# Last feed-forward of a six-layer decoder: relu outputs of the first part kept in SBUF, every fourth group rounded on Pool, norms applied there

## The chip, the cores and the metric

One Trainium2 chip, one core. The metric is the device time of one launch in microseconds, the median of the runs. The core's engines are TensorE (PE; its weight loads stand as PEld in the profile), VectorE (DVE), ScalarE (ACT), GpSimd (Pool, POOL in the profile) and SyncE (SP), which issues the DMAs. They run side by side and wait for one another through semaphores.

## The reference

Six residual layers with a layer norm behind each, on x of 8 batches by 256 rows by 512. The change is in the last of them, a feed-forward with emulated fp8:

```python
def _fp8_matmul(x2d, w):
    scale_x = jnp.maximum(jnp.max(jnp.abs(x2d)) / FP8_MAX, 1e-06)
    scale_w = jnp.maximum(jnp.max(jnp.abs(w)) / FP8_MAX, 1e-06)
    x8 = (x2d / scale_x).astype(jnp.float8_e4m3fn)
    w8 = (w / scale_w).astype(jnp.float8_e4m3fn)
    out = jnp.matmul(x8.astype(x2d.dtype), w8.astype(x2d.dtype).T)
    return out * (scale_x * scale_w)
...
h = _fp8_matmul(x2d, w_fc)
h = jnp.square(jax.nn.relu(h))
out = _fp8_matmul(h, w_proj)
...
x = _layernorm(x + _L1_ffn_ref(x, L1_ffn_w_fc, L1_ffn_w_proj), axis=-1)
```

x2d has 2048 rows and 512 columns, w_fc gives 2048 hidden units, w_proj brings them back to 512 columns. Each product scales by one maximum over its whole input. So the maximum over all of h must be known before the first element of h can be rounded for the second product.

## The kernel before

The layers run one after another; `fp8_ffn_1` is the last. Its weights have been rounded and turned earlier and lie parked in DRAM. It has two parts, each a block of programs, one per engine.

The **first part** finds the maximum of h. The largest element of x comes from a reduction across the partitions on Pool (L2265). Then x is rounded to e4m3 in eight batches of 256 rows: ACT writes `f_x_value` and `f_x_raised` (L2205, L2206), DVE rounds with two instructions (`round_x`, L1122 and L1124), PE turns the result (L2172), ACT copies it to `f_xT` (L2210). Four blocks of 512 rows follow, each of eight groups of 256 hidden units. For a group PE does eight matmuls of 512 columns into two PSUM banks (L2182), and DVE takes the maximum of the 128x1024 result straight from PSUM (L2237); nothing else of it is kept. PE has three bank pairs and waits until DVE has read one. DVE rounds two batches of the next block after the maxima of groups 1 and 4, and PE turns them after its groups 3 and 6. Behind the last group come another reduction across partitions on Pool (L2267) and a chain of one-column instructions on DVE that ends in the scale (L2245 to L2259).

The **second part** goes over the eight batches of 256 rows, with an order made by `slot` and counted out by the class `Plan`. For each group of 256 hidden units it multiplies again on PE (L596, called by `sum_products`), ACT takes the relu and two squares (`f_relu`, `f_value`, `f_raised`: L2316, L2321, L2322), DVE rounds with two instructions (`round_e4m3_above_zero`, L2089 and L2091) into `f_hidden`, and PE multiplies by w_proj (L2304) three groups later. At the end of a batch, for two tiles of 128 rows: DVE adds the product to x (L2345, called fin in the code), takes statistics (L163, L165), Pool makes the root of the variance (`norm_root`, L173 and L175), and DVE applies the norm (`norm_apply`, L180). A finished batch goes out by DMA (L2362).

The two rounding instructions are the same form in every place; the second waits for the first:

```python
    eng.scalar_tensor_tensor(tmp, raised, LEAST, value, ALU.max, ALU.subtract).then_inc(linked, 1)
    eng.wait_ge(linked, n + 1)
    return eng.scalar_tensor_tensor(out, raised, LEAST, tmp, ALU.max, ALU.subtract)
```

Both of its tensors, the bf16 `raised` and the fp32 `value` or `tmp`, lie in SBUF.

## Time and profile before

| | |
|---|---|
| median of 3 runs | 2402.31 us (2401.89 to 2404.9) |
| span of the profiled execution, first to last instruction | 2393.3 us |
| what lies around the span, by the median | 9.0 us |
| last feed-forward in the profiled execution | 2168.3 to 2393.3 us |
| its first part | 2168.3 to 2257.2 us |
| its second part, to the last instruction of DVE | 2257.2 to 2390.1 us |

One execution is profiled; it has no time of its own beside the span. All times of rows are microseconds from the start of that span. A row of a timeline has its start, its duration, the engine, the line of the kernel, the operation, what it writes and reads with the shapes, a count, and in brackets how long the engine had idled and who ended that. A name's buffer number is left out.

### The profile page before, as it was taken

To read this page: it belongs to the slowest core of one execution; us is meant where nothing else is said; L and a number is where in the kernel's file an instruction comes from. 1 tells how busy PE (TensorE), PEld (TensorE's weight loads), DVE (VectorE), ACT (ScalarE), POOL (GpSimd) and SP (SyncE) were. 2 spreads that over 40 slices of the span, in tenths; PEclk is the share of its full clock that TensorE was granted. 3 is DMA by queue.
4 is the path that set the end of the run, shared out by engine and by line. 5 is a ranking of instruction groups with operands and counts; after the bars stand their busy time and mean duration, and the time that the engine had idled before them with its cause. 6 is when DMAs were issued, how large, how long until landed. Compare 5 with 4: busy or idle time off the path is not lost. (4 is left out here: it accounts for less than half of the span.)

```text
span 2393.3 us, 40933 instructions
## 1 busy us (share of the span) xinstructions
PE 2087.9 (87%) x15408; PEld 1781.9 (74%) x15408; DVE 1641.9 (69%) x3731; ACT 1221.2 (51%) x3223; POOL 751.6 (31%) x810
## 2 busy tenths in 40 slices
PE   6999999379899888799978789999999999975897
PEld 5899988267777777577767688889988888962454
DVE  3677777547777776688856655566777676765798
ACT  3656655256766664333433244445555554432397
POOL 1222222376666763344430111111111112220012
PEclk8999999689999998899989899999999999997999
DMA  4111121200000000611110032223324221201001
GB/s 163 54 54 47 48 71 63 77 8 6 5 5 6 6 1 1 229 63 36 36 49 1 2 140 93 85 100 127 118 89 154 89 102 57 77 1 71 1 27 45
DMA packets 50875, 143.95 MB, mean 60 GB/s; under 512 B 4588, under 2 KB 15853, under 8 KB 45688
## 3 DMA queue, kind: packets, MB, share of 16 engines
q1 hardware_dynamic: 50680, 141.34, 16.7%
q8 instruction: 124, 2.03, 0.4%
q14 instruction: 71, 0.58, 0.1%
HBM read 111.95 MB, written 29.36 MB: 59 GB/s over the span
## 5 line engine op out<-in xcount | busy, mean ns | idle before, releaser
L2030 POOL TENSOR_TENSOR x_probs<-x_probs,x_total 128x512 f32<-128x512 f32 x128 | 133.2, 1041 | 588.4 <-DVE x_total L2000 588.2
L1951 ACT ACTIVATE x_probs<-x_probs,x_nmax 128x256 f32<-128x256 f32 x256 | 128.3, 502 | 259.3 <-DVE x_nmax L1990 259.3
L139 DVE TENSOR_TENSOR x_probsT_lo<-banks,x_probsT_hi 128x512 fp32r<-128x512 f32 x256 | 168.0, 682 | 51.8 <-ACT x_probsT_hi L133 51.3
L133 ACT ACTIVATE x_probsT_hi<-banks 128x512 fp32r<-128x512 f32 x256 | 144.9, 603 | 107.8 <-PE banks L1885 83.6
L596 PE MATMUL banks<-x_turned,x_wq_hi 128*128 128x256 f32 x1024 | 185.4, 282 | 9.8 <-DVE x_turned L139 9.8
L596 PE MATMUL banks<-x_probsT_hi,x_V_hi 128*128 128x256 f32 x512 | 151.5, 296 | 33.7 <-DVE x_probsT_lo L139 33.7
L596 PEld LDWEIGHTS banks<-x_turned,x_wq_hi 128*128 128x128 f32 x1024 | 157.0, 189 | 11.0 <-DVE x_turned L139 11.0
L901 POOL TENSOR_TENSOR x_probs<-x_probs,x_total 128x960 f32<-128x960 f32 (+1 forms) x128 | 131.7, 1049 | 92.9 <-DVE x_total L1053 92.9
L588 POOL TENSOR_TENSOR a_probs<-a_probs,a_total 128x512 f32<-128x512 f32 (+1 forms) x64 | 94.9, 1493 | 179.7 <-DVE a_total L558 179.7
L1010 ACT ACTIVATE x_probs<-banks,x_nmax 128x240 f32<-128x240 f32 x256 | 114.8, 467 | 68.6 <-DVE x_nmax L1041 68.6
L596 PE MATMUL banks<-x_probsT_hi,x_V_lo 128*128 128x256 f32 x512 | 147.3, 288 | 0.0
L596 PE MATMUL banks<-x_probsT_lo,x_V_hi 128*128 128x256 f32 x512 | 147.3, 288 | 0.0
L596 PE MATMUL banks<-x_turned,x_wq_lo 128*128 128x256 f32 x512 | 143.5, 280 | 0.0
L1308 POOL TENSOR_TENSOR f_hid_lo<-f_hid,f_hid_hi 128x256 fp32r<-128x256 f32 x128 | 93.9, 734 | 142.0 <-ACT f_hid_hi L133 141.8
L596 PEld LDWEIGHTS banks<-x_probsT_hi,x_V_hi 128*128 128x128 f32 x512 | 100.0, 195 | 43.2 <-DVE x_probsT_lo L139 41.2
L1289 ACT ACTIVATE f_act<-f_z 128x256 f32<-128x256 f32 x128 | 53.4, 417 | 151.1 <-DVE f_z L1360 151.0
L522 ACT ACTIVATE a_probs<-banks,a_nmax 128x128 f32<-128x128 f32 (+1 forms) x256 | 104.3, 425 | 39.9 <-DVE a_nmax L548 39.5
L1271 PE MATMUL banks<-f_downT,f_hid_hi 128*128 128x512 f32 x256 | 111.1, 434 | 1.6 <-POOL f_hid_lo L1308 1.6
L596 PE MATMUL banks<-x_wo_hi,x_oT_hi 128*128 128x512 f32 x256 | 105.0, 410 | 2.6 <-DVE x_oT_lo L139 2.6
L596 PE MATMUL banks<-x_wo_hi,x_oT_lo 128*128 128x512 f32 x256 | 101.0, 395 | 0.0
L596 PE MATMUL banks<-x_wo_lo,x_oT_hi 128*128 128x512 f32 x256 | 101.0, 395 | 0.0
L596 PEld LDWEIGHTS banks<-x_probsT_lo,x_V_hi 128*128 128x128 f32 x512 | 100.3, 196 | 0.9
(450 smaller groups left out, 7146.2 us busy)
## 6 DMA issues: line engine op xcount, KB each, us to landing
x_turned<-x_parked SPq DMA_DIRECT2D x24, 1536.0 KB, 6.6
x_parked<-x_turned SPq DMA_DIRECT2D x8, 1536.0 KB, 5.8
x_raw_q<-in_L_xattn_Wq_dram SPq DMA_DIRECT2D x5, 1024.0 KB, 5.2
x_raw_o<-in_L_xattn_Wo_dram SPq DMA_DIRECT2D x5, 1024.0 KB, 8.4
x_all<-in_x_dram SPq DMA_DIRECT2D x2, 2048.0 KB, 18.0
a_sign_raw<-in_L_ffn_W_g_dram SPq DMA_DIRECT2D x8, 512.0 KB, 3.7
f_parked<-a_sign_turned SPq DMA_DIRECT2D x16, 256.0 KB, 2.4
a_sign_raw<-in_L_ffn_W_u_dram SPq DMA_DIRECT2D x8, 512.0 KB, 3.7
```

The source lines that it names most:

```text
L133: return eng.activation(out, in_, ACT.Copy, scale=scale)
L139: return eng.tensor_tensor(out, in_, high.bitcast(F32), ALU.subtract)
L522: ins = eng.activation(probs[u % NP][:, r, 0:keys], banks[:, r, :], ACT.Exp, bias=nmax[:, u, r:r + 1], accum_out=total[:, u, r:r + 1])
L588: eng.tensor_tensor(probs[u % NP][:, :, 0:keys], probs[u % NP][:, :, 0:keys], total[:, u, :].unsqueeze(2).to_broadcast([P, G4, keys]), ALU ...
L596: ins = eng.matmul(out, lhs, rhs, start=start and n == 0, stop=stop and n == len(steps) - 1)
L901: ins = eng.tensor_tensor(tile, tile, total[:, u, n, :].unsqueeze(2).to_broadcast([P, G4, c1 - c0]), ALU.mult)
L1010: eng.activation(probs[u % NP][:, r, 0:MAIN], g.S[:, r, 0:MAIN], ACT.Exp, bias=nmax[:, u, r:r + 1], accum_out=total[:, u, 0, r:r + 1])
L1271: ins = eng.matmul(g.S[:, 2 * b.parity + t, :], h[:, t * P:(t + 1) * P], downT[:, m, :], start=m == 0 and n == 0, stop=m == HT - 1 and n == 1)
L1289: eng.activation(act[zb][:, :], z[zb][:, :], ACT.Silu).then_inc(silued, 1)
L1308: eng.tensor_tensor(hid_lo[buf][:, :], hid[buf][:, :], hid_hi[buf][:, :].bitcast(F32), ALU.subtract).then_inc(low, 1)
L1951: ins = eng.activation(probs[t][r][:, j, :], probs[t][r][:, j, :], ACT.Exp, bias=nmax[:, t, r, j:j + 1], accum_out=total[:, t, r, j:j + 1])
L2030: eng.tensor_tensor(probs[t][r][:, :, :], probs[t][r][:, :, :], total[:, t, r, :].unsqueeze(2).to_broadcast([P, 2, S]), ALU.mult).then_inc ...
```

## The change

`fp8_ffn_1` is written anew. In the first part ACT takes the relu of every group from PSUM into an SBUF tensor `kept` (128 KB of each partition), PE's banks are freed by that, and DVE takes its maximum from `kept`. The value of x is made by Pool instead of ACT. Both reductions across partitions are done with a diagonal, a matmul with ones and a maximum (`everywhere`) in place of Pool's. w_fc and w_proj share one tensor `weights`; w_proj is loaded at the end of the first part.

The second part has no up-projection. It goes over four blocks of 512 rows by eight groups of 128x1024. ACT squares twice from `kept`. DVE rounds six groups of eight with the same two instructions. Of groups 3 and 7 DVE only does the `max` with `LEAST` (in place, on bf16), and Pool does the two subtractions. Statistics of the block before are taken behind groups 1, 2, 4 and 5 (`FINS`), and Pool makes the root and also applies the norm; for the last block DVE applies it. The semaphores of the norms are shared by all layers, with counts that run on (`so_far`), which changes no order in the other layers.

```diff
-    def __init__(self, prologue, slots, epilogue, events, rings):
+    def __init__(self, prologue, slots, epilogue, events, rings, so_far):
-        total = {e: 0 for e in events}
+        total = {e: so_far.get(e, 0) for e in events}
...
-        gathered, rooting, rooted = g.sem("a1_variance_ready"), g.sem("a1_root_steps"), g.sem("a1_root_ready")
+        gathered, rooting, rooted = g.gathered, g.rooting, g.rooted
...
+    NG = HT // 2
+    NB = B * S // BANK
+    WIDE = 2 * BANK
+    TILES = BANK // P
+    RING = 4
+    FINS = {1: 0, 2: 1, 4: 2, 5: 3}
+    BY_POOL = (3, 7)
+    def pooled(k):
+        return k in BY_POOL
+    def by_pool(u):
+        return sum(pooled(v % NG) for v in range(u))
...
+        kept = sb("kept", [P, NB, NG, WIDE])
+        xT = sb("xT", [P, KD, B * S], BF16)
+        weights = sb("weights", [P, 2, NG * KD * P], BF16)
+        fc = [weights[:, h, :].rearrange("p (m k n) -> p m k n", k=KD, n=P) for h in range(2)]
+        proj = [weights[:, h, :].rearrange("p (c m n) -> p c m n", c=D // P, n=P) for h in range(2)]
         pairs = [g.S[:, 0:2, :], g.S[:, 2:4, :], g.R[:, 0:2, :]]
+        last = kept[:, NB - 1, :, :]
+        value = [last[:, i, :] for i in range(2)]
+        raised, rounded = ([last[:, at, :].bitcast(BF16)[:, i * WIDE:(i + 1) * WIDE] for i in range(2)] for at in (2, 3))
...
+                half = KD * P * NG
+                for h in range(2):
+                    eng.dma_start(weights[:, h, :], parked[:, h * half:(h + 1) * half]).then_inc(w_loaded[h], 16)
+                rows = parked[:, 2 * half:4 * half].rearrange("p (c m n) -> p c (m n)", c=D // P, m=HT)
+                for h in range(2):
+                    eng.wait_ge(up_full, (NB - 1) * NG + (h + 1) * NG // 2)
+                    eng.dma_start(weights[:, h, :].rearrange("p (c n) -> p c n", c=D // P),
+                                  rows[:, :, h * NG * P:(h + 1) * NG * P]).then_inc(w_loaded[h], 16)
...
                 def group(n, k):
                     use = n * NG + k
                     if use >= 3:
-                        eng.wait_ge(up_free, use - 2)
+                        eng.wait_ge(up_kept, use - 2)
+                    h, m = divmod(2 * k, NG)
                     for j in range(2):
-                        m = 2 * k + j
                         for kt in range(KD):
-                            ins = eng.matmul(pairs[use % 3][:, j, :], fcT[:, m, kt, :], xT[:, kt, n * BANK:(n + 1) * BANK],
+                            ins = eng.matmul(pairs[use % 3][:, j, :], fc[h][:, m + j, kt, :], xT[:, kt, n * BANK:(n + 1) * BANK],
                                              start=kt == 0, stop=kt == KD - 1)
                     ins.then_inc(up_full, 1)
+                def spread_top(n, bank):
+                    eng.wait_ge(topped, 3 * n - 1)
+                    eng.matmul(bank, ones[:, :], diag[:, :], start=True, stop=True).then_inc(spread, 1)
+                eng.wait_ge(filled, 1)
+                spread_top(1, g.S[:, 0, 0:P])
                 turn(0)
...
-                def scale_x(c):
+                def raise_x(c):
                     if c == 0:
                     if c >= 2:
                         eng.wait_ge(xrounded, c - 1)
-                    src = g.x[:, c * QT * D:(c + 1) * QT * D]
-                    eng.activation(value[c % 2][:, :], src, ACT.Copy, scale=w8.inverse[:, 0:1])
-                    eng.activation(raised[c % 2][:, :], src, ACT.Abs, scale=w8.raise_by[:, 0:1]).then_inc(valued, 1)
+                    eng.activation(raised[c % 2], x_of(c), ACT.Abs, scale=w8.raise_by[:, 0:1]).then_inc(raised_s, 1)
...
-                for c in range(B):
-                    scale_x(c)
-                    if c >= 1:
-                        copy_x(c - 1)
-                copy_x(B - 1)
+                raise_x(0)
+                raise_x(1)
+                copy_x(0)
+                copy_x(1)
+                raise_x(2)
+                raise_x(3)
+                for n in range(NB):
+                    for k in range(NG):
+                        use = n * NG + k
+                        eng.wait_ge(up_full, use + 1)
+                        eng.activation(kept[:, n, k, :], pairs[use % 3].rearrange("p j n -> p (j n)"), ACT.Relu).then_inc(up_kept, 1)
+                        if n < NB - 1 and k in (4, 6):
+                            copy_x(2 * n + 2 + (k == 6))
+                        if n < NB - 2 and k in (5, 7):
+                            raise_x(2 * n + 4 + (k == 7))
...
+                def everywhere(n, bank, top, source):
+                    eng.tensor_reduce(amax[:, top:top + 1], source, AX.X, ALU.max).then_inc(topped, 1)
+                    eng.wait_ge(topped, 3 * n - 2)
+                    eng.tensor_scalar(diag[:, :], g.ident[:, :], amax[:, top:top + 1], None, ALU.mult).then_inc(topped, 1)
+                    eng.wait_ge(spread, n)
+                    eng.tensor_reduce(scaled[:, top:top + 1], bank, AX.X, ALU.max).then_inc(topped, 1)
+                    eng.wait_ge(topped, 3 * n)
                 eng.wait_ge(w8.x_topped, B)
-                eng.tensor_reduce(amax[:, 0:1], w8.x_tops[:, :], AX.X, ALU.max).then_inc(topped, 1)
-                eng.wait_ge(reduced, 1)
+                everywhere(1, g.S[:, 0, 0:P], 0, w8.x_tops[:, :])
...
                 for use in range(total):
                     n, k = divmod(use, NG)
-                    eng.wait_ge(up_full, use + 1)
-                    eng.tensor_reduce(hmax[:, use:use + 1], pairs[use % 3].rearrange("p j n -> p (j n)"), AX.X,
-                                      ALU.max).then_inc(up_free, 1)
+                    eng.wait_ge(up_kept, use + 1)
+                    eng.tensor_reduce(hmax[:, use:use + 1], kept[:, n, k, :], AX.X, ALU.max).then_inc(up_max, 1)
                     if n < NB - 1 and k in (1, 4):
                         round_x(2 * n + 2 + (k == 4))
...
             def _(eng):
-                eng.wait_ge(topped, 1)
-                eng.partition_all_reduce(scaled[:, 0:1], amax[:, 0:1], P, RED.max).then_inc(reduced, 1)
-                eng.wait_ge(topped, 2)
-                eng.partition_all_reduce(scaled[:, 3:4], amax[:, 3:4], P, RED.max).then_inc(reduced, 1)
-        relu = [sb(f"relu{i}", [P, BANK]) for i in range(NZ)]
-        value = [sb(f"value{i}", [P, BANK]) for i in range(NZ)]
-        raised = [sb(f"raised{i}", [P, BANK], BF16) for i in range(NZ)]
-        tmp = [sb(f"tmp{i}", [P, BANK]) for i in range(NZ)]
+                eng.memset(ones[:, :], 1.0).then_inc(filled, 1)
+                for c in range(B):
+                    if c == 0:
+                        eng.wait_ge(w8.linked, 6)
+                    if c >= 2:
+                        eng.wait_ge(xrounded, c - 1)
+                    eng.tensor_scalar(value[c % 2], x_of(c), w8.inverse[:, 0:1], None, ALU.mult).then_inc(valued, 1)
+        turning = xT[:, :, :].rearrange("p k n -> p (k n)")
+        raised, hidden = ([turning[:, (first + i) * WIDE:(first + i + 1) * WIDE] for i in range(RING)] for first in (0, RING))
...
+        def accumulator(n, t):
+            return (g.S if n % 2 else g.R)[:, t, :]
+                for u in range(NB * NG):
+                    n, k = divmod(u, NG)
+                    if k == 0 and n >= 2:
+                    wait_rounded(eng, u)
+                    h, m = divmod(2 * k, NG)
+                    for t in range(TILES):
                         for j in range(2):
-                            ins = eng.matmul(g.S[:, 2 * b.parity + t, :], h[:, j, t * P:(t + 1) * P], projT[:, :, 2 * m + j, :],
-                                             start=m == 0 and j == 0, stop=m == HT // 2 - 1 and j == 1)
+                            at = j * BANK + t * P
+                            ins = eng.matmul(accumulator(n, t), hidden[u % RING][:, at:at + P], proj[h][:, :, m + j, :],
+                                             start=k == 0 and j == 0, stop=k == NG - 1 and j == 1)
                     ins.then_inc(downed, 1)
...
+                for u in range(NB * NG):
+                    group = kept[:, u // NG, u % NG, :]
+                    if u >= RING:
+                        wait_rounded(eng, u - RING)
+                    eng.activation(raised[u % RING], group, ACT.Square, scale=raise_root)
+                    eng.activation(group, group, ACT.Square, scale=root).then_inc(squared, 1)
...
+                links = 0
+                for u in range(NB * NG):
+                    n, k = divmod(u, NG)
+                    group, raise_to = kept[:, n, k, :], raised[u % RING]
+                    eng.wait_ge(squared, u + 1)
+                    if pooled(k):
+                        eng.tensor_scalar(raise_to, raise_to, LEAST, None, ALU.max).then_inc(capped, 1)
+                    else:
+                        eng.scalar_tensor_tensor(group, raise_to, LEAST, group, ALU.max, ALU.subtract).then_inc(linked, 1)
+                        links += 1
+                        if u >= RING:
+                            eng.wait_ge(downed, u - RING + 1)
+                        eng.wait_ge(linked, links)
+                        eng.scalar_tensor_tensor(hidden[u % RING], raise_to, LEAST, group, ALU.max, ALU.subtract).then_inc(rounded_v, 1)
+                    if n and k in FINS:
+                        fin(n - 1, FINS[k])
...
+            @block.gpsimd
+            def _(eng):
+                def root_of(n, t):
+                    done = TILES * n + t
+                    eng.wait_ge(gathered, before["stats"] + done + 1)
+                    norm_root(eng, rooting, before["rooting"] + POOL_ROOT_STEPS * done, st[t], 1e-5, g.minus_half[:, :]).then_inc(rooted, 1)
+                    eng.wait_ge(rooted, before["root"] + done + 1)
+                for u in range(NB * NG):
+                    n, k = divmod(u, NG)
+                    if pooled(k):
+                        group, raise_to, n_before = kept[:, n, k, :], raised[u % RING], by_pool(u)
+                        eng.wait_ge(capped, n_before + 1)
+                        eng.tensor_tensor(group, raise_to, group, ALU.subtract).then_inc(pool_linked, 1)
+                        if u >= RING:
+                            eng.wait_ge(downed, u - RING + 1)
+                        eng.wait_ge(pool_linked, n_before + 1)
+                        eng.tensor_tensor(hidden[u % RING], raise_to, group, ALU.subtract).then_inc(rounded_p, 1)
+                    if n and k in FINS:
+                        t = FINS[k]
+                        root_of(n - 1, t)
+                        norm_apply(eng, x_tile(n - 1, t), x_tile(n - 1, t), st[t]).then_inc(applied_p, 1)
+                for t in range(TILES):
+                    root_of(NB - 1, t)
...
+                for b in range(B):
+                    n, half = divmod(b, 2)
+                    if n < NB - 1:
+                        eng.wait_ge(applied_p, QT * (b + 1))
+                    else:
+                        eng.wait_ge(applied_v, QT * (half + 1))
```

POOL, second part, from its start to the second group 7. `f_xT` holds the buffers `raised` and `hidden`, `f_kept` the relu outputs, `f_st` the statistics. Before:

```order
L173 TENSOR_SCALAR f_st<-f_st 128x1
L175 TENSOR_TENSOR f_st<-f_st,minus_half 128x1
L173 TENSOR_SCALAR f_st<-f_st 128x1
L175 TENSOR_TENSOR f_st<-f_st,minus_half 128x1
```

Of the change:

```order
L2387 TENSOR_TENSOR f_kept<-f_xT,f_kept 128x1024
L2391 TENSOR_TENSOR f_xT<-f_xT,f_kept 128x1024
L174 TENSOR_SCALAR f_st<-f_st 128x1
L176 TENSOR_TENSOR f_st<-f_st,minus_half 128x1
L181 TENSOR_SCALAR x_all<-x_all,f_st 128x512
L174 TENSOR_SCALAR f_st<-f_st 128x1
L176 TENSOR_TENSOR f_st<-f_st,minus_half 128x1
L181 TENSOR_SCALAR x_all<-x_all,f_st 128x512
L2387 TENSOR_TENSOR f_kept<-f_xT,f_kept 128x1024
L2391 TENSOR_TENSOR f_xT<-f_xT,f_kept 128x1024
```

Pool had 32 small instructions in this part; it has 16 of 128x1024 and 12 of 128x512 besides.

DVE, second part, a stretch around the end of a group 7 and the first statistics of the block before. Before, at the end of a batch:

```order
L2089 SCALAR_TENSOR_TENSOR f_tmp<-f_raised,f_value 128x512
L2091 SCALAR_TENSOR_TENSOR f_hidden<-f_raised,f_tmp 128x512
L2345 SCALAR_TENSOR_TENSOR x_all<-banks,f_scaled,x_all 128x512
L163 BN_STATS f_st<-x_all 128x6
L165 BN_AGGR f_st<-f_st 128x2
```

Of the change, from the first `max` alone of a group 7 on:

```order
L2356 TENSOR_SCALAR f_xT<-f_xT 128x1024
L2358 SCALAR_TENSOR_TENSOR f_kept<-f_xT,f_kept 128x1024
L2363 SCALAR_TENSOR_TENSOR f_xT<-f_xT,f_kept 128x1024
L2358 SCALAR_TENSOR_TENSOR f_kept<-f_xT,f_kept 128x1024
L2363 SCALAR_TENSOR_TENSOR f_xT<-f_xT,f_kept 128x1024
L2343 SCALAR_TENSOR_TENSOR x_all<-banks,f_scaled,x_all 128x512
L164 BN_STATS f_st<-x_all 128x6
L166 BN_AGGR f_st<-f_st 128x2
```

Between the `max` of group 7 and the statistics that need that group's product now stand the two groups 0 and 1 of the next block.

ACT, first part, from the sixth relu of a block on (`f_kept<-x_all` is the raised x, in the last block's place). Before:

```order
L2205 ACTIVATE f_x_value<-x_all,f_inverse 128x1024
L2206 ACTIVATE f_x_raised<-x_all,f_raise_by 128x1024
L2210 ACTIVATE f_xT<-banks 128x4x256
```

Of the change:

```order
L2222 ACTIVATE f_kept<-banks 128x1024 x5
L2209 ACTIVATE f_xT<-banks 128x4x256
L2222 ACTIVATE f_kept<-banks 128x1024
L2205 ACTIVATE f_kept<-x_all,f_raise_by 128x1024
L2222 ACTIVATE f_kept<-banks 128x1024
L2209 ACTIVATE f_xT<-banks 128x4x256
```

The relus of the groups stand between PE and DVE, and between the copies that PE waits for.

## Rows read from the trace of the kernel before

**Rows 1.** Busy time by stretch: us, each engine's busy time (instructions), granted clock, DMA.

```profile
2189.30:2253.50 64.20, 60.77 (x304) 27.65 (x304) 52.27 (x45) 16.46 (x16) 0.00 (x0) 0.97 0.00 1
...
2261.50:2385.00 123.50, 113.77 (x750) 70.86 (x748) 113.84 (x184) 108.59 (x189) 22.40 (x28) 0.99 0.07 26
```

**Rows 2.** Timeline of all engines, start of the first part.

```profile
2168.33 0.16 DVE L2228 TENSOR_REDUCE f_amax<-f_x_tops 128x1 f32<-128x8 f32 x1 [0.33 <-PEq L1779]
...
2178.44 0.38 POOL L2265 PARTITION_ALL_REDUCE f_scaled<-f_amax  x1 [13.27 <-issue]
...
2179.42 1.15 ACT L2205 ACTIVATE f_x_value<-x_all,f_inverse 128x1024 f32<-128x1024 f32 x1 [23.79 <-DVE f_raise_by L1117]
```

**Rows 3.** Timeline of all engines, blocks of the first part.

```profile
2197.08 1.22 DVE L1124 SCALAR_TENSOR_TENSOR f_x_rounded<-f_x_raised,f_x_value 128x1024 bf16<-128x1024 bf16 x1
...
2198.45 0.61 PE L2172 MATMUL banks<-ident,f_x_rounded 128*128 128x128 bf16 x8 [0.34 <-DVE f_x_rounded L1124]
...
2236.47 15.70 PE L2182 MATMUL banks<-f_xT,f_fcT 128*128 128x512 bf16 x72
```

**Rows 4.** Instructions that write or read f_diag: duration ns min/median/max.

```profile
L1251 PE MATMUL banks<-f_diag,f_ones x32: 275/328/528, 968.7 to 1194.4; 128*128 128x128 f32 x32
L1345 DVE TENSOR_SCALAR f_diag<-ident,f_inv x16: 285/286/288, 967.5 to 1190.8; 128x128 f32<-128x128 f32 x16
```

**Rows 5.** Timeline of DVE, end of the first part and second part.

```profile
2254.14 0.16 DVE L2245 TENSOR_TENSOR f_scaled<-f_scale 128x1 f32<-128x1 f32 x1 [0.49 <-POOL f_scaled L2267]
...
2261.50 0.69 DVE L2089 SCALAR_TENSOR_TENSOR f_tmp<-f_raised,f_value 128x512 f32<-128x512 bf16 x1 [4.35 <-ACT f_raised L2322]
...
2282.15 0.74 DVE L2345 SCALAR_TENSOR_TENSOR x_all<-banks,f_scaled,x_all 128x512 f32<-128x512 f32 x1
...
2283.77 0.69 DVE L2089 SCALAR_TENSOR_TENSOR f_tmp<-f_raised,f_value 128x512 f32<-128x512 bf16 x1
```

**Rows 6.** Timeline of all engines, the last statistics and the last norm.

```profile
2385.08 0.75 DVE L2345 SCALAR_TENSOR_TENSOR x_all<-banks,f_scaled,x_all 128x512 f32<-128x512 f32 x1 [0.72 <-PE banks L2304]
...
2389.55 0.55 DVE L180 TENSOR_SCALAR x_all<-x_all,f_st 128x512 f32<-128x512 f32 x1 [0.77 <-POOL f_st L175]
```

**Rows 7.** Groups of Pool's instructions by form, whole span: busy us, mean ns.

```profile
L139 POOL TENSOR_TENSOR x_wdv_lo<-x_raw_d,x_wdv_hi 128x1024 fp32r<-128x1024 f32 x1 | 2.4, 2354 | 0.0
...
L779 POOL MEMSET x_bias<- 128x512 f32 x1 | 0.5, 524 | 0.9 <-POOLq L324 0.9
```

**Rows 8.** Timelines of Pool and of DVE at 60 us, first layer.

```profile
60.17 1.42 POOL L588 TENSOR_TENSOR a_probs<-a_probs,a_total 128x512 f32<-128x512 f32 x1 [7.32 <-DVE a_total L558]
...
60.01 0.68 DVE L541 TENSOR_SCALAR a_sign_of<-a_sign_raw 128x1024 bf16<-128x1024 f32 x1
60.73 1.94 DVE L543 SCALAR_TENSOR_TENSOR a_sign_of<-a_sign_raw,a_sign_of 128x1024 bf16<-128x1024 f32 x1
```

**Rows 9.** Timelines of Pool and of DVE at 466 us, second layer.

```profile
466.53 6.30 POOL L139 TENSOR_TENSOR x_wo_lo<-x_raw_o,x_wo_hi 128x2048 fp32r<-128x2048 f32 x1 [8.18 <-ACT x_wo_hi L133]
...
466.12 1.21 DVE L139 TENSOR_TENSOR x_wk_lo<-x_raw_kv,x_wk_hi 128x1024 fp32r<-128x1024 f32 x1
467.25 1.21 DVE L139 TENSOR_TENSOR x_wdk_lo<-x_raw_d,x_wdk_hi 128x1024 fp32r<-128x1024 f32 x1
```

**Rows 10.** Timelines of Pool and of DVE in the second part.

```profile
2287.57 0.99 POOL L175 TENSOR_TENSOR f_st<-f_st,minus_half 128x1 f32<-128x1 f32 x1
...
2287.45 0.69 DVE L2091 SCALAR_TENSOR_TENSOR f_hidden<-f_raised,f_tmp 128x512 bf16<-128x512 bf16 x1
2288.05 0.68 DVE L2089 SCALAR_TENSOR_TENSOR f_tmp<-f_raised,f_value 128x512 f32<-128x512 bf16 x1
```

**Rows 11.** Line 139 on DVE, one input in PSUM: duration ns min/median/max.

```profile
L139 DVE TENSOR_TENSOR x_probsT_lo<-banks,x_probsT_hi x256: 637/683/693, 513.8 to 2151.3; 128x512 fp32r<-128x512 f32 x128
```

**Rows 12.** Busy time by stretch, columns as in the first group.

```profile
2380.50:2383.90 3.40, 3.24 (x8) 0.99 (x8) 3.24 (x7) 0.00 (x0) 0.53 (x1) 0.51 0.00 0
```

**Rows 13.** Timeline of PE in that stretch.

```profile
2380.66 4.38 PE L2304 MATMUL banks<-f_projT,f_hidden 128*128 128x512 bf16 x12 [1.91 <-DVE f_hidden L2091]
```

More of the change, by code:

```diff
@@ L321, in self_attention_0 @@
                 "root": {"out": 1}, "link": {"rec": 1, "out": STATISTICS_STEPS, "fin": 1}},
-        rings={"R": (4, {kind: lambda *a, kind=kind: turn[(kind, *a)] for kind in ring}), "S": (1, {"score": lambda m, qt: 0})})
+        rings={"R": (4, {kind: lambda *a, kind=kind: turn[(kind, *a)] for kind in ring}), "S": (1, {"score": lambda m, qt: 0})}, so_far=g.norms_so_far)
     with ExitStack() as mem:
@@ L2141, in fp8_ffn_1 @@
         hlinked = g.sem("f1_hmax_link")
-        fc_loaded, proj_loaded = [g.sem(f"f1_parked_fc_loaded{m}") for m in range(2)], g.sem("f1_parked_proj_loaded")
-        topped, reduced, valued = g.sem("f1_top_ready"), g.sem("f1_top_reduced"), g.sem("f1_x_scaled")
+        w_loaded = [g.sem(f"f1_parked_loaded{h}") for h in range(2)]
+        topped, spread = g.sem("f1_top_ready"), g.sem("f1_top_spread")
+        valued, raised_s = g.sem("f1_x_scaled"), g.sem("f1_x_raised")
         xlinked, xrounded, turned, copied = (g.sem("f1_x_" + n) for n in ("link", "rounded", "turned", "copied"))
-        with ExitStack() as raws:
-            def ring(name, dt):
-                return [raws.enter_context(nc.sbuf_tensor(f"f1_x_{name}{i}", [P, QT * D], dt)) for i in range(2)]
-            value, raised, rounded = ring("value", F32), ring("raised", BF16), ring("rounded", BF16)
-            block = raws.enter_context(nc.Block())
+        last = kept[:, NB - 1, :, :]
@@ L2152, in _, with x_of @@
+        value = [last[:, i, :] for i in range(2)]
+        raised, rounded = ([last[:, at, :].bitcast(BF16)[:, i * WIDE:(i + 1) * WIDE] for i in range(2)] for at in (2, 3))
+        def x_of(c):
+            return g.x[:, c * QT * D:(c + 1) * QT * D]
+        with nc.Block() as block:
             @block.sync
@@ L2279, in fp8_ffn_1 @@
-        block = mem.enter_context(nc.Block())
-        @block.tensor
-        def _(eng):
-            def do(job, b):
-                kind, a = job[0], job[2:]
-                if kind == "up":
-                    m, = a
-                    if (count := plan.freed("R", "relu", b, "up", m)) is not None:
-                        eng.wait_ge(relued, count)
-                    bank = g.R[:, plan.buf("R", b, "up", m), :]
-                    for j in range(2):
-                        ins = sum_products(eng, bank[:, j * S:(j + 1) * S],
-                                           [(fcT[:, 2 * m + j, kt, :], xT[:, kt, b.columns(1, 0, S)])
-                                            for kt in range(KD)])
-                    ins.then_inc(full, 1)
-                if kind == "down":
-                    m, = a
-                    if (b.c, m) == (0, 0):
-                        eng.wait_ge(proj_loaded, 16)
-                    eng.wait_ge(rounded, plan.done("round", b, "up", m))
-                    h = hidden[plan.buf("H", b, "up", m)]
-                    for t in range(QT):
+                eng.memset(ones[:, :], 1.0).then_inc(filled, 1)
@@ new lines, in fp8_ffn_1 @@
+        st = [sb(f"st{t}", [P, 12]) for t in range(TILES)]
+        gathered, rooting, rooted = g.gathered, g.rooting, g.rooted
+        before = dict(g.norms_so_far)
+        squared, capped = g.sem("f1_square_ready"), g.sem("f1_raised_capped")
+        linked, pool_linked = g.sem("f1_link"), g.sem("f1_pool_link")
+        rounded_v, rounded_p = g.sem("f1_rounded_by_vector"), g.sem("f1_rounded_by_pool")
+        downed, summed, stats = g.sem("f1_down_added"), g.sem("f1_sum_ready"), g.sem("f1_stats_link")
@@ new lines, in fp8_ffn_1 @@
+        with nc.Block() as block:
+            @block.tensor
+            def _(eng):
+                for u in range(NB * NG):
+                    n, k = divmod(u, NG)
+                    if k == 0 and n >= 2:
+                        eng.wait_ge(summed, TILES * (n - 1))
+                    if u in (0, NG // 2):
+                        eng.wait_ge(w_loaded[u // (NG // 2)], 32)
+                    wait_rounded(eng, u)
+                    h, m = divmod(2 * k, NG)
+                    for t in range(TILES):
@@ new lines, in _ @@
+            @block.gpsimd
+            def _(eng):
+                def root_of(n, t):
[17 more added lines that the diff above has]
+                        norm_apply(eng, x_tile(n - 1, t), x_tile(n - 1, t), st[t]).then_inc(applied_p, 1)
+                for t in range(TILES):
+                    root_of(NB - 1, t)
```

174 lines of the change are left out of this document (55 added, 119 removed).

## Prediction

> **What bounds it now.** I read the busy time by stretch first, then the timelines at the two parts' starts and ends, then every place where Pool and DVE work side by side. In the first part PE bounds: 60.77 of 64.20 us [rows 1]. A block of 512 rows takes 15.70 us for its 72 matmuls [rows 3], 1.74 for a group's eight; DVE is busy for 52.27 and ACT for 16.46, so ACT has room. Ahead of it stands a dead stretch: DVE has the maximum per partition at 2168.49, Pool's reduction only starts at 2178.44 although nothing in the trace holds it but "issue", and ACT's first instruction comes at 2179.42 [rows 2]. In the second part no engine bounds alone: DVE 113.84, PE 113.77, ACT 108.59 of 123.50 us [rows 1]. The change takes half of PE's work away there and nothing of DVE's, so what counts is DVE, and what Pool's new work does to it.
>
> **First part.** *Start.* Before, 2168.33 to 2179.42 is 11.1 us [rows 2]. Now: maximum 0.16, diagonal 0.29, matmul 0.53 (slowest of its kind), the maximum of its 128 columns about as the diagonal, 0.29 [rows 4], handovers between engines estimated at 0.45 together, and from there to ACT's first instruction 0.6, as now from 2178.82 to 2179.42: 2.3 us. Minus 8.8. Nothing hides that stretch, so all of it comes off.
>
> *Relu in the way.* DVE's rounding of x stands behind the maxima of groups 1 and 4, and the maximum now waits for a relu instead of PE's end. The nearest row for a relu of 128x1024 is ACT's 1.15 [rows 2]; with a handover of 0.1 the rounding comes 1.25 later. PE already waits 0.34 for the rounding at a turn [rows 3], so there is no slack to absorb it: six turns, plus 7.5. The last maximum is as much later: plus 1.25. Together +8.75. Bounds: the third bank pair lets PE swallow half of it (+4.4), or an x copy on ACT ahead of the relu adds about 1.0 a turn (+14.8).
>
> *Value on Pool, 128x1024.* The trace has no such instruction. The nearest are 0.52 for a 128x512 memset, twice that 1.04, and 2.35 for a two-input 128x1024 [rows 7]. I take 1.04: the rounding is then late only by its relu; at 2.35 the first batch costs about 2.5 once more.
>
> *Second reduction.* DVE's own maximum takes 0.16 as at the start, it waits 0.49 for Pool's and goes on at 2254.14 [rows 5], about 0.7 with the start; the new way takes 1.55 by the terms of the first, and one more column instruction 0.2: +1.05. First part: −8.8 + 8.75 + 1.05 = **+1.0**.
>
> **Second part.** It takes 132.95 us now, from 2257.15, 4.35 ahead of DVE's first rounding [rows 5], to the end of the last norm at 2390.10 [rows 6].
>
> *A pair of roundings* of 128x1024: one takes 1.22 [rows 3], the second waits for the first (1.25 to its start), and an independent follower starts 0.09 before the end (0.69 long, next one 0.60 later [rows 10]): 1.25 + 1.14 = 2.39 a group. The `max` alone is nearest to the 0.68 of a 128x1024 conversion [rows 8], 0.6 net; 1.22 is its upper bound, four microseconds over the part.
>
> *Pool against DVE.* This is the term that decides. At 60 us a two-input DVE instruction took 1.94, not 1.22, and ended 1.08 after Pool's end, while Pool's 128x512 took 1.42 and ended 0.90 after DVE's previous end [rows 8]: one waited whole for the other, both ways. At 466 us Pool's 128x2048 stood through two DVE instructions, to 468.46, then took 4.37, so 2.19 for 128x1024 [rows 9]. A DVE instruction with one input in PSUM never shows it (637 to 693 over 256 of them [rows 11]). The rounding pair has two inputs in SBUF, and it stands right beside Pool's. I therefore price each Pool subtraction as 2.2 us taken from DVE, not as work beside it. The nearest rows for the duration are 2.35 [rows 7] and 2.19. Bounds: nothing, and 2.35 plus a wait.
>
> *Pool's norms* (128x512) are bounded by the memset's 0.52 [rows 7] and the 1.42 of a two-input instruction that had to wait [rows 8]. They come when DVE is at the product's addition (PSUM input) and the statistics, which do not collide; four roots and norms get 0.3 a block.
>
> *A period of a block on DVE*: six pairs 14.3, two `max` 1.2, four statistics of 1.62 (2282.15 to 2283.77 [rows 5]) 6.5, own sum 22.0; four holds by Pool of 2.2, 8.8; four handovers of 0.1, 0.4; norms 0.3. And one wait: the first statistics need group 7's product. From its `max`: a rounding that got in first 1.2, subtraction 2.2, two more roundings in between 2.3, subtraction 2.2, eight matmuls 1.74 or 3.24, start 0.35 [rows 3], 10.0 to 11.5 us; DVE fills 4.8 (two pairs) and 4.4 (two holds) of it, so 0.8 to 2.3 stay, 1.5 taken. P = **33.0**. The 3.24 is what eight matmuls of 512 columns took at a granted 0.51, the lower level of 1.2 GHz [rows 12], behind 1.91 us of idling [rows 13]; PE now works 14 of 33 us in short pieces, so I expect the lower level for part of the time.
>
> *Sum.* To DVE's first instruction two squares of 1.15 and starts, 2.8 (4.35 before, with the up-projection [rows 5]). Block 0 to its last `max`: 14.3 + 1.2 + 4.4 = 19.9. Three periods, 99.0. After the last `max` two subtractions 4.8, matmuls 2.6, start 0.5: 7.9. The end: from the first of two last additions to the end of the last norm now 2385.08 to 2390.10, 5.0 [rows 6]; four tiles need two more statistics, 3.2, and two more norms, 1.0: 9.2. Together 138.8, against 132.95: **+5.85**. With the first part +6.85. The profiled span of 2393.3 and 9.0 around it make the median, so the forecast is 2402.3 + 6.9 = **2409**.
>
> The Trainium skill ("SBUF — State Buffer", section "SBUF: two separate sides") says that the shared port pair is an exclusive lock: a DVE instruction with two SBUF inputs or a GpSimd one, whichever starts first, holds it for its whole length. Rows 8 agree with that; rows 9, where Pool stood through a second DVE instruction as well, go beyond it. By the page's order alone the sum would be rival one's.
>
> **Rivals.** *One, a fair exchange and PE at 2.4 GHz*: Pool gets in at each gap between dependent roundings, as the small instruction at 2287.57 did: it waited for the rounding that had begun at 2287.45, and the next one was not delayed (0.68) [rows 10]. P is then 22.0 + 8.8 = 30.8, three times 2.2 less: **2402.6**, no change. For it: the pair has such a gap in every group. Against: the wait for group 7 has to vanish.
> *Two, DVE keeps the pair*: Pool waits through back-to-back roundings as in rows 9 (1.9 each time), its groups come late, ring and statistics wait; P about 36: **2418**.
> *Three, faster: Pool subtracts with a bf16 input at half the price*, 1.2 instead of 2.35 [rows 7]; sixteen subtractions by 1.15 are 18.4: **2391**. No row has this mix of types on Pool; that two inputs cost Pool over four times a memset of half the size speaks against it, since reading two inputs is what stays. It ends faster as soon as a hold is under 1.5 us.
> *Four, no exclusion for this form*: the roundings stay at 1.22 beside Pool; P = 22.0 + 2.1 of waits = 24.1, 26.7 off over three periods and 4.4 in block 0: **2378**. Rows 8 speak plainly against it.
>
> **How the numbers follow.** Forecast (2404 to 2414 with its own unknowns) 0.44, one 0.24, two 0.12, three 0.13, four 0.07. About 0.2% (4.8 us) is what a measurement can tell from no change: 2397.5 to 2407.1. Three, four and a little of one's spread are faster, 0.22; one and the lower edge of the forecast are the same, 0.34; the rest is slower, 0.44. The range leaves out case four and the far end of two: 2386 to 2420.
>
> **What would show it.** The scales stand near 2170.5 instead of 2179.4. A block of the first part lasts near 18.2, with PE waiting about 1.6 at each turn. In the second part DVE's rounding of 128x1024 has a mean well above 1.22, up to 3.4 beside a subtraction, and Pool's subtractions 2.2 to 3.5. The first statistics of neighbouring blocks lie 33 apart, and PE's granted clock falls below 0.9. The prediction is wrong if roundings stay at 1.22 beside Pool, if Pool's subtraction is near 1.2, or if the relu's delay vanishes in PE's three bank pairs.

## The result, and the profile after

The changed kernel takes 2409.53 us (median of 8 runs, 2404.91 to 2413.0) against 2402.11 (8 runs). The ratio is 1.0033, 95% interval 1.0021 to 1.0046: slower by 7.4 us, where 6.9 were forecast. Taken from the last feed-forward alone (from the first top reduction on DVE to DVE's last instruction) it grew from 221.77 us (2168.33 to 2390.10) to 229.79 (2174.89 to 2404.68), so by 8.0.

The profiled run lasted 2409.82 for a span of 2407.9, so 1.9 us lie around the span and not 9.0: the profiled execution of before was a quick one. Its last layer began at 2168.33; behind the same earlier layers it began between 2168.9 and 2175.0 in the eleven executions profiled here afterwards. In the 400 us from 500 on their granted clock lies between 0.94 and 0.97, but a late start goes with a low clock only in part of them, so what spreads the earlier layers stays open here. So the layer is compared below by its own stretches.

Busy time by stretch, columns as in [rows 1]. First the second part of before, over its whole length:

```profile
2257.20:2390.10 132.90, 117.61 (x768) 73.60 (x768) 117.96 (x192) 110.45 (x192) 24.18 (x32) 0.96 0.08 29
```

Then the two parts after:

```profile
2189.90:2261.30 71.40, 60.40 (x297) 27.56 (x302) 52.06 (x44) 43.56 (x44) 12.25 (x5) 0.97 0.06 18
2266.30:2404.70 138.40, 68.83 (x256) 26.91 (x256) 100.03 (x108) 67.71 (x64) 96.21 (x60) 0.80 0.07 27
```

In the second part PE lost 49 us of work and DVE 18, and yet it is 5.4 us longer. Pool went from 24.18 to 96.21 us, and the granted clock from 0.96 to 0.80.

The start of the first part, timeline of all engines, answering [rows 2]:

```profile
2174.89 0.16 DVE L2238 TENSOR_REDUCE f_amax<-f_x_tops 128x1 f32<-128x8 f32 x1 [0.32 <-PEq L1780]
...
2177.23 2.19 ACT L2205 ACTIVATE f_kept<-x_all,f_raise_by 128x1024 bf16<-128x1024 f32 x2 [17.81 <-DVE f_raise_by L1118]
2177.31 13.47 POOL L2286 TENSOR_SCALAR f_kept<-x_all,f_inverse 128x1024 f32<-128x1024 f32 x4 [2.25 <-DVE f_raise_by L1118]
2180.21 1.23 DVE L1123 SCALAR_TENSOR_TENSOR f_kept<-f_kept 128x1024 f32<-128x1024 bf16 x1 [3.01 <-POOL f_kept L2286]
...
2189.92 8.73 PE L2176 MATMUL banks<-f_xT,f_weights 128*128 128x512 bf16 x31 [1.52 <-ACT f_xT L2209]
...
2200.04 0.61 PE L2166 MATMUL banks<-ident,f_kept 128*128 128x128 bf16 x8 [1.40 <-DVE f_kept L1125]
...
2217.86 0.61 PE L2166 MATMUL banks<-ident,f_kept 128*128 128x128 bf16 x8 [1.40 <-DVE f_kept L1125]
```

ACT starts 2.34 us after the top reduction instead of 11.09. But DVE then idles for Pool's value of x (3.01). The last two rows are the turns behind group 3 of two neighbouring blocks, 17.82 apart, and PE waits 1.40 at each turn where it waited 0.34 [rows 3]. Before, the second of these turns came 15.72 after the one in [rows 3]:

```profile
2214.17 0.61 PE L2172 MATMUL banks<-ident,f_x_rounded 128*128 128x128 bf16 x8 [0.35 <-DVE f_x_rounded L1124]
```

Second part, the end of the second block, first Pool's timeline, then DVE's:

```profile
2314.39 1.58 POOL L176 TENSOR_TENSOR f_st<-f_st,minus_half 128x1 f32<-128x1 f32 x1
2316.08 2.09 POOL L181 TENSOR_SCALAR x_all<-x_all,f_st 128x512 f32<-128x512 f32 x1
2318.14 0.64 POOL L174 TENSOR_SCALAR f_st<-f_st 128x1 f32<-128x1 f32 x1
2318.86 1.59 POOL L176 TENSOR_TENSOR f_st<-f_st,minus_half 128x1 f32<-128x1 f32 x1
2320.56 2.55 POOL L181 TENSOR_SCALAR x_all<-x_all,f_st 128x512 f32<-128x512 f32 x1
2323.08 2.13 POOL L2387 TENSOR_TENSOR f_kept<-f_xT,f_kept 128x1024 f32<-128x1024 bf16 x1
2325.35 2.13 POOL L2391 TENSOR_TENSOR f_xT<-f_xT,f_kept 128x1024 bf16<-128x1024 bf16 x1
```

```profile
2315.46 0.42 DVE L2356 TENSOR_SCALAR f_xT<-f_xT 128x1024 bf16<-128x1024 bf16 x1
...
2330.79 0.75 DVE L2343 SCALAR_TENSOR_TENSOR x_all<-banks,f_scaled,x_all 128x512 f32<-128x512 f32 x1 [7.92 <-PE banks L2326]
```

Read them together: DVE's `max` of group 7 is done at 2315.88. Pool's subtractions of it begin only at 2323.08, because two norms and a root stand ahead of them in Pool's queue. PE's product follows, and DVE has idled 7.92 us before the first addition (L2343) that leads to the statistics. Across the part, groups of instructions by line (count, then busy us, mean ns):

```profile
L2363 DVE SCALAR_TENSOR_TENSOR f_xT<-f_xT,f_kept 128x1024 bf16<-128x1024 bf16 x24 | 38.9, 1622 | 2.3
L2358 DVE SCALAR_TENSOR_TENSOR f_kept<-f_xT,f_kept 128x1024 f32<-128x1024 bf16 x24 | 33.4, 1393 | 6.6 <-ACT f_kept L2337 6.6
L181 POOL TENSOR_SCALAR x_all<-x_all,f_st 128x512 f32<-128x512 f32 x12 | 26.0, 2163 | 1.3
L2343 DVE SCALAR_TENSOR_TENSOR x_all<-banks,f_scaled,x_all 128x512 f32<-128x512 f32 x16 | 11.9, 743 | 27.6 <-PE banks L2326 27.6
```

Forty-eight roundings at 1.22 are 58.6 us; they took 72.3, so 13.7 us of lengthening. DVE's waits for PE ahead of L2343 are 27.6. The chain that ended last, shares of the span by line:

```profile
POOL x_all L181 1%; POOL f_st L176 1%; POOL f_xT L2391 1%; POOL f_kept L2387 1%; POOL f_st L174 0%; DVE f_xT L2363 0%; DVE f_kept L2358 0%; PE banks L2326 0%; ACT f_xT L2336 0%; ACT f_kept L2337 0%; DVE x_all L2343 0%; DVE f_st L164 0%; DVE x_all L181 0%; DVE f_st L166 0%; DVE f_xT L2356 0%
```

Its five largest lines are all Pool's, and the norm comes first, which the prediction had at 0.3 us a block together with the roots.

### The profile page after: what moved, and what is told of

It reads as the page before. It is cut to its first block and busy times, and to the rows that moved or that the text cites. A ratio compares the mean times of both kernels' runs of the same rounds, so it can differ in the third digit from the quotient of the medians.

```text
span 2407.9 us, 39685 instructions
## 1 busy us (share of the span) xinstructions
PE 2051.9 (85%) x14893; PEld 1747.1 (73%) x14900; DVE 1620.2 (67%) x3652; ACT 1201.7 (50%) x3119; POOL 847.3 (35%) x845
## 3 DMA queue, kind: packets, MB, share of 16 engines
q8 instruction: 120, 1.97, 0.3%
## 5 line engine op out<-in xcount | busy, mean ns | idle before, releaser
L2326 PE MATMUL banks<-f_weights,f_xT 128*128 128x512 bf16 x256 | 68.8, 433 | 64.0 <-POOL f_xT L2391 52.4
L2326 PEld LDWEIGHTS banks<-f_weights,f_xT 128*128 128x128 bf16 x256 | 26.9, 109 | 105.7 <-POOL f_xT L2391 56.3
```

Source lines behind the costliest of these rows:

```text
L2326: ins = eng.matmul(accumulator(n, t), hidden[u % RING][:, at:at + P], proj[h][:, :, m + j, :], start=k == 0 and j == 0, stop=k == NG - 1 a ...
```

## The experiments

The forecast had one mechanism for the second part: Pool's subtractions hold DVE's two-input roundings up (below: exclusion). The trace after suggests another beside it: Pool runs its instructions in order, and what DVE waits for stands behind norms and roots (below: the queue theory). The first four runs set one against the other. "Second part" below is from the end of the scales to DVE's last instruction (138.40 in the changed kernel).

### DVE applies the norms, Pool still rounds

```diff
                     if n and k in FINS:
                         fin(n - 1, FINS[k])
+                        if FINS[k]:
+                            apply(n - 1, FINS[k] - 1)
+                    if n and k == 6:
+                        apply(n - 1, TILES - 1)
...
                         root_of(n - 1, t)
-                        norm_apply(eng, x_tile(n - 1, t), x_tile(n - 1, t), st[t]).then_inc(applied_p, 1)
```

> The change, but DVE applies every norm (0.52 us each by its rows); Pool keeps the roots and the subtractions of groups 3 and 7. Theory, Pool's queue: the second part is set by what stands in Pool's queue ahead of group 7's subtractions (roots of 1.6, norms of 2.08), so DVE idles 7.9 us in each block; without the norms the period of a block falls from 34.0 to about 29, the idle time to 2 or less, and the time to about 2390. Rival, exclusion: DVE is set by the roundings that Pool's subtractions hold up; these stay, so the period stays at 33 or above and the time at 2404 to 2410.

2398.59 us (before on the same chip 2400.65; ratio 0.9994, 0.9983 to 1.0006), second part 128.24. So 10.2 us came back although DVE does 12 norms more (6.3 us). By line:

```profile
L2362 DVE SCALAR_TENSOR_TENSOR f_kept<-f_xT,f_kept 128x1024 f32<-128x1024 bf16 x24 | 42.1, 1755 | 3.5 <-ACT f_kept L2337 3.5
L2367 DVE SCALAR_TENSOR_TENSOR f_xT<-f_xT,f_kept 128x1024 bf16<-128x1024 bf16 x24 | 36.4, 1516 | 2.3
L2343 DVE SCALAR_TENSOR_TENSOR x_all<-banks,f_scaled,x_all 128x512 f32<-128x512 f32 x16 | 11.9, 745 | 8.6 <-PE banks L2326 8.6
```

The wait for PE fell from 27.6 to 8.6, as the queue theory says, but the roundings are lengthened more, 78.5 − 58.6 = 19.9 instead of 13.7: what had been a wait turned partly into a hold. The time lies between the two expectations (2390, and 2404 to 2410): neither theory alone is right.

### DVE rounds everything; with and without Pool's norms

```diff
-    BY_POOL = (3, 7)
+    BY_POOL = ()
```

> The change, but DVE rounds all eight groups; Pool keeps roots and norms. Pool's queue: nothing waits for Pool's subtractions; DVE's own work of a block is 8 x 2.39 + 6.5 = 25.6, with some collisions a period of about 27, time about 2385. Exclusion: the twelve norms of 2.08 and their roots hold the roundings up for their whole length, the period is 25.6 + 4 x 2.1 or more = 34, the time about 2405.

> The change, but DVE rounds all groups and applies all norms; Pool makes only the roots. Both theories: DVE's own 25.6 + 4 x 0.52 = 27.7 a block, time about 2386. Pool's queue: within 4 us of the run in which Pool keeps the norms alone. Exclusion: about 20 faster than that run.

With Pool's norms: 2381.27 us (ratio 0.9927, 0.9909 to 0.9946), second part 114.53. With the norms on DVE (this edit and the one above): 2386.93 (0.9951, 0.9933 to 0.997), second part 116.94. Taking the rounding from Pool is worth 23.9 us of the changed kernel's second part. Pool's norms, harmful with it, do no harm without it: the second part is 2.4 us shorter with them, though the intervals of the two ratios overlap, and DVE's roundings are hardly lengthened (mean 1297 and 1208 ns). Exclusion's forecast for the first of the two runs, 2405, is far off, so a Pool norm is not priced like a subtraction.

### A Pool load that nobody waits for

Neither rounding nor norms on Pool, and beside groups 3 and 7 two instructions on spare tensors:

```diff
...
+                    if k in (3, 7):
+                        eng.wait_ge(squared, u + 1)
+                        for i in range(2):
+                            eng.wait_ge(spared, 2 + 2 * (2 * n + k // 4) + i)
+                            eng.tensor_tensor(spare[:, :], spare16[:, :], spare[:, :], ALU.subtract).then_inc(spared, 1)
...
```

> As the run with neither on Pool, plus two subtractions of 128x1024 on Pool beside groups 3 and 7 on spare tensors whose result nobody waits for: the hold by itself, without the wait. Exclusion in full: sixteen instructions of 2.13 that DVE waits for whole, +30 to +34 over the run without them. Pool's queue: DVE's roundings are lengthened as in the changed kernel (13.5 us in all over its 48), +8 to +16. No exclusion: 0 to +2.

2417.96 us (ratio 1.0077, 1.0051 to 1.0102), second part 148.39. Against 116.94 that is 31.45 us, 1.97 for each of sixteen instructions whose results nobody uses. Below, groups by line without the load (two rows) and with it (three rows):

```profile
L2367 DVE SCALAR_TENSOR_TENSOR f_xT<-f_xT,f_kept 128x1024 bf16<-128x1024 bf16 x32 | 39.2, 1225 | 3.0
L2362 DVE SCALAR_TENSOR_TENSOR f_kept<-f_xT,f_kept 128x1024 f32<-128x1024 bf16 x32 | 38.9, 1216 | 2.7 <-ACT f_kept L2337 2.7
```

```profile
L2364 DVE SCALAR_TENSOR_TENSOR f_kept<-f_xT,f_kept 128x1024 f32<-128x1024 bf16 x32 | 54.4, 1701 | 2.7 <-ACT f_kept L2339 2.7
L2369 DVE SCALAR_TENSOR_TENSOR f_xT<-f_xT,f_kept 128x1024 bf16<-128x1024 bf16 x32 | 48.0, 1500 | 3.0
L2400 POOL TENSOR_TENSOR f_spare<-f_spare 128x1024 f32<-128x1024 bf16 x16 | 43.7, 2733 | 11.2 <-ACT f_kept L2339 10.1
```

DVE's instructions are the same; 24.3 us of the difference lie in longer roundings, most of the rest in DVE's norms (mean 865 ns instead of 522), none in a wait for Pool. That is exclusion in full, near the price the forecast had used. It is not confined to DVE's two-input instructions: a norm of DVE has one tensor input, and one that began beside the load took 2.37 us instead of 0.52:

```profile
2321.87 5.11 POOL L2400 TENSOR_TENSOR f_spare<-f_spare 128x1024 f32<-128x1024 bf16 x2
2322.62 2.37 DVE L181 TENSOR_SCALAR x_all<-x_all,f_st 128x512 f32<-128x512 f32 x1
```

### The same load with one input

```diff
-                            eng.tensor_tensor(spare[:, :], spare16[:, :], spare[:, :], ALU.subtract).then_inc(spared, 1)
+                            eng.tensor_scalar(spare[:, :], spare16[:, :], 1.0, None, ALU.mult).then_inc(spared, 1)
```

> As the run with a Pool load that nobody needs, but with instructions of one input (128x1024, 2.8 us each by the first part's rows) in place of two. If any Pool instruction that reads SBUF holds a two-input DVE instruction for its whole length: +40 or more over the run with neither on Pool (2387). If only Pool's two-input form does: +6 or less, for the odd collisions of 0.4 to 0.7 seen beside the norms.

2398.29 us (ratio 0.999, 0.9974 to 1.0006), second part 126.30: 9.4 us over the run without a load, 0.58 for each instruction. The profiled execution took 2391.04 and its last layer began at 2168.91, earlier than in the other runs, so it is the second parts that are compared and not the medians.

```profile
L2400 POOL TENSOR_SCALAR f_spare<-f_spare 128x1024 f32<-128x1024 bf16 x16 | 54.7, 3419 | 9.3 <-ACT f_kept L2339 8.1
L2364 DVE SCALAR_TENSOR_TENSOR f_kept<-f_xT,f_kept 128x1024 f32<-128x1024 bf16 x32 | 44.8, 1399 | 2.7 <-ACT f_kept L2339 2.7
```

Each runs longer on Pool than a subtraction (3.42 us), yet costs DVE a third. So of these two forms it is the subtraction that shuts DVE out whole; the one-input form costs more than the 6 us allowed for it, but nothing like 40. Whether the second input makes the difference or the kind of instruction is not separated here: both changed together. It fits that Pool's norms, which have one tensor input, cost little when they stand alone.

### Only the order in Pool's queue

```diff
-                    if n and k in FINS:
-                        t = FINS[k]
+                    for t in {1: (0,), 2: (1,), 7: (2, 3)}.get(k, ()) if n else ():
```

> The change with one thing moved in Pool's queue: the roots and norms of the third and fourth tile of the block before stand behind the two subtractions of group 7 instead of ahead of them. Pool's work is the same to the instruction. Pool's queue: group 7's subtractions start some 5 us earlier, DVE's idle time falls from 35 us to 15 or 20, the second part from 138 to 142 to about 126 to 130, the time to about 2400. Exclusion alone: DVE has lost no less, nothing moves beyond 3 us.

2400.1 us, beside the changed kernel once more:

> The changed kernel itself once more, beside the run above. Its second part came out at 138.4, and the same second part behind two other first parts at 142.3 and 140.6, with a granted clock of PE of 0.8 and of 0.7 to 0.75; so its second part should lie between 138 and 143, and its time at 2405 to 2413.

2409.36 us (ratio 1.0041, 1.0026 to 1.0056), second part 139.52, both as expected. With nothing but the order moved the second part is 131.29, 8.2 us less, and the time 9.3 less. Pool's timeline in the reordered kernel:

```profile
2312.58 2.14 POOL L2387 TENSOR_TENSOR f_kept<-f_xT,f_kept 128x1024 f32<-128x1024 bf16 x1 [2.83 <-DVE f_xT L2356]
2314.87 2.94 POOL L2391 TENSOR_TENSOR f_xT<-f_xT,f_kept 128x1024 bf16<-128x1024 bf16 x1
```

and two of its groups on DVE:

```profile
L2343 DVE SCALAR_TENSOR_TENSOR x_all<-banks,f_scaled,x_all 128x512 f32<-128x512 f32 x16 | 11.9, 744 | 8.3 <-PE banks L2326 8.3
...
L2356 DVE TENSOR_SCALAR f_xT<-f_xT 128x1024 bf16<-128x1024 bf16 x8 | 3.3, 412 | 8.5 <-ACT f_kept L2337 8.5
```

The subtraction of group 7 starts when its `max` ends (2312.50), and the wait for PE falls from 27.6 to 8.3. The queue theory is shown. Not all of the idle time comes back: 8.5 us of a new wait for ACT's squares stand before the `max`, and roundings are lengthened by 16.3 instead of 13.7. The second part ends 1.3 us above the 126 to 130 that were expected, the time where it was expected.

### The first part

```diff
+                    eng.activation(value[c % 2], x_of(c), ACT.Copy, scale=w8.inverse[:, 0:1]).then_inc(valued, 1)
                     eng.activation(raised[c % 2], x_of(c), ACT.Abs, scale=w8.raise_by[:, 0:1]).then_inc(raised_s, 1)
...
-                    eng.tensor_scalar(value[c % 2], x_of(c), w8.inverse[:, 0:1], None, ALU.mult).then_inc(valued, 1)
```

> The change, but ACT makes the value of x ahead of the raised copy, as before the change. If Pool's 3.4 us for each of the first values is what makes the start 2.8 us longer than the sum had it, the stretch from the first top reduction to the first maximum of a group falls from 19.3 to 16.5 us and nothing else moves; time about 2407. Rival: ACT's two extra instructions of 1.1 stand in the way of relus, the block of the first part grows from 17.8 to over 18.5, and the gain is gone.

2412.21 us (ratio 1.0051, 1.0033 to 1.0068). The first group begins 12.11 us after the top reduction instead of 15.03, the first maximum 16.75 instead of 19.31: the 2.6 to 2.9 us are there. But the last maximum ends 85.94 after it, against 86.44: 2.4 of them are gone again, since ACT's added instructions delay relus and PE waits 2.05 instead of 1.40 at two turns. The rival is right. The second part, untouched, took 142.32 at a granted clock of 0.70 to 0.75 in its blocks (0.78 to 0.83 in the changed kernel's), which is where the 2.7 us that the median rose by lie.

```diff
-                    if n < NB - 1 and k in (1, 4):
-                        round_x(2 * n + 2 + (k == 4))
+                    if n < NB - 1 and k in (0, 3):
+                        round_x(2 * n + 2 + (k == 3))
```

> The value on ACT, and DVE rounds x behind the maxima of groups 0 and 3 instead of 1 and 4. If the relu's delay of the rounding is what PE waits for (1.40 at each of six turns), the wait goes to 0.3 or less, a block of the first part falls from 17.8 to about 15.7, 6 to 8 us less than with the value on ACT alone; about 2399. Rival: the delay is in the bank pairs (PE waits for relus), so the wait moves to the groups and the block stays at 17 or more.

With this and the value on ACT: 2402.28 us (ratio 1.0012, 1.0001 to 1.0024), 9.9 less than with the value on ACT alone; 6.7 of them lie in the first part and 1.7 in the second. The last maximum ends 79.23 after the top reduction, 6.7 earlier. PE's timeline at the turns:

```profile
2201.39 0.61 PE L2166 MATMUL banks<-ident,f_kept 128*128 128x128 bf16 x8
...
2212.58 0.61 PE L2166 MATMUL banks<-ident,f_kept 128*128 128x128 bf16 x8 [0.56 <-DVE f_kept L1125]
```

Four of six turns wait for nothing, two for 0.56. Two blocks open with about 1.1 us of waiting for ACT's copy instead, so a block stays at 16.8 and not 15.7. That PE waited for a rounding that came late is shown; the wait is not fully gone.

### The best of them together

DVE rounds all groups, Pool keeps roots and norms, the value of x on ACT, the rounding one group earlier.

> DVE rounds all groups, Pool keeps roots and norms, the value of x is on ACT, the rounding of x stands one group earlier. By the terms: 2381 less 2.8 less 6 to 8, about 2371. Rival: with the first part shorter nothing else changes, since the parts are separated by the maximum over all of h; it only fails if one of the two edits fails by itself.

2375.55 us, ratio 0.9895 (0.9875 to 0.9915) to the kernel before, with the layer at 198.46 us (221.77 before): first part to the scales 83.97, second 114.49. Its layer is 31 us shorter than the changed kernel's and 23 shorter than before. The time misses the 2371 expected by 4.5: the first part gave 6.8 in all and not 9 to 11, and the last layer began 1.1 later than in the run with the rounding on DVE, from which the 2371 was worked out.

## Why the prediction was right, and where it was right for the wrong reason

The sum hit: 2409 forecast, 2409.5 measured, from a first part of +2.6 (forecast +1.0) and a second of +5.45 (forecast +5.85). Step by step:

- *Start*: −8.75, forecast −8.8. Right to the handover.
- *Value on Pool*: forecast at no cost, taken as 1.04 us with 2.35 as the dearer row. It takes 2.84 with little beside it, mean 3.11, so the way from the scales to the first group grew from 9.90 to 12.69: +2.8, near the 2.5 that the prediction gave for 2.35. This term of the first part was mis-sized: what was measured lies above both rows. The nearest row by size (a memset) was the wrong kind.
- *Relu in the way*: +7.3, forecast +8.75. The waits at the turns grew by 1.06 each, not 1.25; the relu takes 1.02, not 1.15. Moving the rounding showed that this is the place. (The 15.70 of [rows 3], read in the prediction as one block, is the last group of one block and the eight of the next; a block with its turns took 15.72, so nothing hangs on it.)
- *Second reduction*: +1.23, forecast +1.05.
- *Second part*: by the terms of the sum, to DVE's first instruction 2.73 us (forecast 2.8); block 0 to the end of its last `max` 19.27 (19.9); three periods of 27.58, 33.97 and 34.05, together 95.6 (three of 33.0, 99.0); from there to the last additions 11.70 (7.9); the end 9.08 (9.2). That makes 138.4 for 138.8, from these rows of DVE and the one at 2315.46 above:

```profile
2269.03 1.23 DVE L2358 SCALAR_TENSOR_TENSOR f_kept<-f_xT,f_kept 128x1024 f32<-128x1024 bf16 x1 [2.74 <-ACT f_kept L2337]
...
2287.88 0.42 DVE L2356 TENSOR_SCALAR f_xT<-f_xT 128x1024 bf16<-128x1024 bf16 x1
...
2349.43 0.42 DVE L2356 TENSOR_SCALAR f_xT<-f_xT 128x1024 bf16<-128x1024 bf16 x1
...
2383.48 0.42 DVE L2356 TENSOR_SCALAR f_xT<-f_xT 128x1024 bf16<-128x1024 bf16 x1
2395.60 0.75 DVE L2343 SCALAR_TENSOR_TENSOR x_all<-banks,f_scaled,x_all 128x512 f32<-128x512 f32 x1 [11.70 <-PE banks L2326]
```

  So the hit is luck: the periods were priced 3.4 us too long and the wait at the end 3.8 too short. The forecast of a period had 8.8 us of holds and 1.5 of waiting for group 7. In the first period no norm stands ahead of group 7 in Pool's queue; DVE waits for nothing there, and its roundings are 5.8 us longer. In the one from 2330.79 to 2364.84 (first addition to first addition) the roundings beside Pool are 2.5 us longer and DVE idles 9.6. The failing step is the sentence that four roots and norms get 0.3 a block, and its bounds of 0.52 and 1.42: a norm takes 2.08 even where no rounding runs beside it (mean 2.16), a root 0.23 + 0.57 alone but up to 1.2 + 1.6 where it waits for roundings. In that period four roots (9.8) and four norms (8.8) fill 18.6 of Pool's 34 us, the four subtractions 9.3 more; Pool's queue became what sets the period, and group 7 stands last in it. The two errors cancelled: the wait was larger than priced, and the holds were smaller, since the two subtractions of group 7 (2323.08 to 2327.48) ran while DVE was waiting for them. (In the first period the holds were already under 8.8, because part of group 3's subtractions ran beside an addition and statistics, which took no longer for it.)
- *The price of one hold* was right: 2.2 forecast, 1.97 measured where nothing else is in the way. Rival four is out. Rival three (half the price with a bf16 input) is out too: the subtraction takes 2.13 with DVE idle. Rival one's vanishing wait came only in the first period. In rival two DVE would have kept Pool waiting; what delayed Pool's groups was its own queue.
- *The lock rule* of the Trainium skill ("SBUF — State Buffer", "SBUF: two separate sides") is borne out for two-input instructions on both sides by the spare load, 1.97 us lost for each 2.13. It makes no difference between Pool's forms, and the run with one input does: 0.58 us for an instruction of 3.42.
- *PE's clock*: forecast below 0.9, it was 0.80. The same second part stands in four of the profiled executions: at 0.80, 0.79, 0.77 and 0.72 it took 138.40, 139.52, 140.63 and 142.32. The two go together; what sets the clock was not tested.

What the change cost and gave, by the runs: without Pool's rounding and norms its second part is 116.94, 16 us under the kernel before. Pool's rounding adds 11.3 to that (about 16 of DVE's work saved; 19.9 of longer roundings and 6.6 more of waiting for PE in return), and the norms in the same queue another 10.2. The 16 us that the second part would have gained without either were given back, and 5.5 more.

## What to carry to other kernels

Work moved to Pool is only free if it doesn't hold DVE up: each two-input subtraction on Pool cost DVE 1.97 us where it took 2.13 alone, so eight groups taken off DVE made the second part 11.3 us longer. Before moving several kinds of work to one in-order engine, write its queue down in order with durations from the same kind of instruction, and ask who waits for the last in it. A sum can come out right with two wrong terms; check the forecast's terms against the trace, not its total.

## What was not expected of the hardware

On Pool a one-input 128x512 norm takes 2.08 us, nearly as long as a two-input subtraction of twice its size (2.13), and a one-input 128x1024 product takes longer than it: at least 2.84 (fp32) or 2.98 (from bf16, beside DVE's roundings). By size and number of inputs one would order them the other way. Beside that subtraction even a one-input norm on DVE took 2.37 us instead of 0.52. The `max` alone on bf16 took 0.42, not the 0.68 of the fp32 row nearest to it.
